# A four-layer gated stack: split fp32r scores for the eight-headed layer, weights of two stages in the streamed buffer, and a new common order of steps

## What is computed

```python
x = x + tanh(g_xattn[0]) * L0_xattn(layernorm(x), ctx)    # 32 heads of 8, differential softmax
x = x + tanh(g_ffn[0])   * L0_ffn(layernorm(x))           # three cycles of a small coupling net
x = x + tanh(g_xattn[1]) * L1_xattn(ctx, layernorm(x), mask)
x = x + tanh(g_ffn[1])   * L1_ffn(layernorm(x))           # 2 shared and 8 routed experts
x = x + tanh(g_xattn[2]) * L2_xattn(layernorm(x), ctx, ctx)
x = x + tanh(g_ffn[2])   * L2_ffn(layernorm(x))           # attention, then 8 experts
x = x + tanh(g_xattn[3]) * L3_xattn(layernorm(x), ctx, ctx)
x = x + tanh(g_ffn[3])   * L3_ffn(layernorm(x))           # quantised weights
```

```python
sim = einsum('bhid,bhjd->bhij', q * scale, k) * scale
sim = where(full_mask, sim, max_neg); attn = softmax(sim); out = attn @ v; out = layernorm(out @ Wo)
```

## Time and profile before

| | us |
|---|---|
| median of 3 runs | 5636.66 (5631.06 to 5639.46) |
| the profiled execution's own time | 5660.27 |
| its span, first to last instruction | 5658.5 |
| PE busy | 4888.0 (86%) |
| DVE busy | 2758.3 (49%) |
| ACT busy | 1853.5 (33%) |
| mean granted TensorE clock | 0.921 of full |

### The profile page before, as it was taken

The page is one execution under the profiler, slowest core; times in us unless marked ns, Lnnn a source line. Parts: engine busy times, 40 slices in busy tenths (PEclk is TensorE's granted clock), DMA queues, the critical chain, the costliest instruction groups (busy, mean ns, idle before and its releaser), DMA issues.

```text
span 5658.5 us, 74258 instructions
## 1 busy us (share of the span) xinstructions
PE 4888.0 (86%) x29184; PEld 3477.8 (61%) x29184; DVE 2758.3 (49%) x7346; ACT 1853.5 (33%) x3068; POOL 95.5 (2%) x180
## 2 busy tenths in 40 slices
PE   2898878989799897998979988899888998889988
PEld 1556765567656685565855658556585565855657
DVE  3535455354553545436454454544545445454454
ACT  2422324233242333423233242332424324242242
POOL 0000000000000000000000000000000000000000
PEclk9898989999899898998989989799897998989989
DMA  6000210002000020000200002000020000200002
GB/s 273 1 1 22 88 50 1 1 22 112 26 1 1 22 112 26 1 9 21 105 26 1 15 23 97 26 1 14 31 90 26 1 22 23 90 26 1 22 23 94
DMA packets 47155, 218.95 MB, mean 39 GB/s; under 512 B 4544, under 2 KB 16832, under 8 KB 27072
## 3 DMA queue, kind: packets, MB, share of 16 engines
q1 hardware_dynamic: 46784, 213.90, 10.2%
HBM read 192.91 MB, written 20.97 MB: 38 GB/s over the span
## 4 chain that ended last, share of the span: by engine, by line
PE 70%; DVE 19%; ACT 5%; issue 3%; DMA 2%; SPq 0%; POOL 0%; DVEq 0%; ACTq 0%
PE w L418 16%; PE w L428 10%; DVE mx L1023 6%; PE o L559 6%; PE w L675 6%; PE w L517 5%; PE w L667 4%; PE w L408 4%; PE w L531 4%; PE o L552 4%; PE w L484 2%; ACT oth L786 2%; PE w L534 1%; PE w L571 1%; PE w L467 1%
## 5 line engine op out<-in xcount | busy, mean ns | idle before, releaser
L824 ACT ACTIVATE pt<-w 128x1024 f32<-128x1024 f32 x640 | 653.8, 1024 | 768.6 <-PE w L534 440.4
L1023 DVE TENSOR_REDUCE mx<-w 128x4 f32<-128x1024 f32 x512 | 593.7, 1218 | 171.9 <-PE w L467 155.1
L559 PE MATMUL o<-pt,va 128*32 128x256 f32 x4096 | 559.5, 410 | 18.7 <-ACT pt L824 18.7
L786 ACT ACTIVATE oth<-w,res 128x256 f32<-128x256 f32 x656 | 264.1, 475 | 731.0 <-PE w L667 599.8
L1259 DVE TENSOR_REDUCE mx<-w 128x2 f32<-128x1024 f32 x128 | 156.9, 1226 | 527.0 <-PE w L519 527.0
L418 PE MATMUL w<-xnT,res 128*128 128x256 f32 x1408 | 375.3, 418 | 33.8 <-ACT xnT L778 24.5
L667 PE MATMUL w<-qsp,ksp 128*128 128x256 f32 x2048 | 350.3, 289 | 0.0
L418 PEld LDWEIGHTS w<-xnT,res 128*128 128x128 f32 x1408 | 281.3, 208 | 98.8 <-issue 47.6
L559 PEld LDWEIGHTS o<-pt,va 128*32 128x32 f32 x4096 | 207.9, 114 | 194.1 <-issue 67.8
L467 PE MATMUL w<-ksp,qsp 32*128 32x256 f32 (+1 forms) x2048 | 260.9, 401 | 73.5 <-DVE mx L1023 41.5
L418 PE MATMUL w<-xnT,stream 128*128 128x256 f32 x1280 | 311.8, 391 | 0.0
(11 more groups left out here) (235 smaller groups left out, 7506.6 us busy)
## 6 DMA issues: line engine op xcount, KB each, us to landing
stream_lo<-split SPq DMA_DIRECT2D x64, 1024.0 KB, 4.8
ksp<-split SPq DMA_DIRECT2D x64, 1024.0 KB, 6.9
stream<-in_moe_dram SPq DMA_DIRECT2D x80, 384.0 KB, 3.6
va<-in_moe_dram SPq DMA_DIRECT2D x8, 1024.0 KB, 10.3
split<-ksp SPq DMA_DIRECT2D x8, 1024.0 KB, 5.6
split<-qsp SPq DMA_DIRECT2D x8, 1024.0 KB, 8.0
res<-in_resident_dram SPq DMA_DIRECT2D x1, 8157.5 KB, 22.1
cx<-in_ctx_dram SPq DMA_DIRECT2D x16, 256.0 KB, 3.6
```

What stands on the lines that cost most here:

```text
L559: mm = pe.matmul(o[g:g + 32, 0:T], by_heads(plan, s)[:, kt, plan.v_of(h), :], pt[:, n % EXPS, a * 512 + kt * T:a * 512 + (kt + 1) * T], st ...
L786: h = act.activation(dst[:, c, :], w[:, c * T:(c + 1) * T], func, bias=bias[:, c:c + 1], **more)
L824: act.activation(pt[:, n % EXPS, :], w[:, :], ACT.Exp, scale=scale).then_inc(S["s_P"], 1)
L1023: dve.tensor_reduce(mx[s][:, :, 2 * u:2 * u + 2].rearrange("p t a -> p a t"), w[:, :].rearrange("p (a t k) -> p a t k", a=2, t=TT), AX_X, ...
```

## The change: what it does

Three things at once.

**Scores of L1.** `q` and `k` are split into a high part (rounded to fp32r) and the rest. For each head, `k1` now holds 128 rows: 64 of high and 64 of low parts (for odd heads the other way round). `qsp` holds the high part of `q` twice, and the low part stands in `hl` (even heads) or `qodd` (odd heads) beside 64 rows of zeros. Two fp32r matmuls of 128 rows take the place of each fp32 matmul. The mask's row and the row of ones become 128-row tiles with zeros in the others (`first_row`, `maskb`). The copies out of PSUM work on 64 partitions at a time: ACT does four for `q` and two each for `kc` and `kl`; DVE then does two subtractions for each, and one memset for `q`. `max` waits for the DVE parts.

**Where weights lie.** `l1_wkv`, `l1_wq` and `l1_wo` (2 MB) leave `res` and are loaded into `stream` in every pass, behind `cx` and ahead of `x` in SP's queue. f1's first five experts go to `stream` when the L1 steps that read the place are done in both slots. `f3_w1` (1 MB) is loaded into `stream` when the last f2 experts are done in both slots, and `f3.h` waits for it.

**The order.** `l1.q` comes after `l1.kl` and `l1.vl`, and `ORDER` is another string. Waits for a reused bank or exponential buffer, so far by count, now name the step that read that buffer. ACT's part of `l3.k` now also waits for the same slot's last `f2.exp`, and PE's `l1.kl` for `l1.xT`.

The core of the diff:

```diff
-    "1016110156106000006006000005000600050550550005000500050500000550050550500500505050005000500555055055"
...
+    "1666166016015151000500000500005000000000000505005005005050500505050050500000500505005005505505500555"
+    "5005555055555550555555555050550205552050500550002205507500005500055505505050705555005505077005050005"
+    "0055050500555000055050000050055555050005555550550550555555550500050505080085055555550005555000555500"
+    "0500500585355503303000080500050550050005005050050055000505005505505505555005050055550005555555505000"
+    "0550505050505000000050500500500505050500555050005555055545055505555509050555505055055050500550505050"
+    "055005555055900005055450055500500050"
...
+        + steps_of(s, "f0.add", "l1.ln", "l1.xT", "l1.kl", "l1.vl", "l1.q") + scores(L1, s) + values(L1, s)
...
                     for tt in range(TT):
-                        pe.matmul(w[:, tt * 512:(tt + 1) * 512], qz[s][:, u, tt * P:(tt + 1) * P],
-                                  k1[s][:, u // 2, :], start=True, stop=False)
-                        mm = pe.matmul(w[:, tt * 512:tt * 512 + T], ones_row[:, 0:P], maskb[s][:, :], start=False, stop=True)
+                        for n, q in enumerate((qsp[s][:, u, :], q_low(s, u))):
+                            pe.matmul(w[:, tt * 512:(tt + 1) * 512], q[:, tt * P:(tt + 1) * P], k1[s][:, u, :],
+                                      start=(n == 0), stop=False)
+                        mm = pe.matmul(w[:, tt * 512:tt * 512 + T], first_row[:, 0:P], maskb[s][:, :], start=False, stop=True)
...
                     for kt in range(KT):
                         o = w[:, kt * T:(kt + 1) * T]
-                        pe.matmul(o, k1[s][:, u // 2, kt * P:(kt + 1) * P], qz[s][:, u, :], start=True, stop=False)
+                        for n, q in enumerate((qsp[s][:, u, :], q_low(s, u))):
+                            pe.matmul(o, k1[s][:, u, kt * P:(kt + 1) * P], q, start=(n == 0), stop=False)
                         if kt < TT:
-                            pe.matmul(o, maskb[s][:, kt * P:(kt + 1) * P], ones_row[:, :], start=False, stop=False)
+                            pe.matmul(o, maskb[s][:, kt * P:(kt + 1) * P], first_row[:, :], start=False, stop=False)
                         mm = pe.matmul(o, sel1[:, u, :], mT[s][:, :], start=False, stop=True)
...
                     elif step == "l1.q":
                         w = full(act, step, s)
-                        for half in range(2):
-                            h = act.activation(qz[s][:, half::2, :], chunks_of(w, 4), ACT.Copy, scale=W_["half"][:, half:half + 1])
-                        h.then_inc(S["s_qz"], 1)
+                        full(act, "l1.cT", s)
+                        for odd in range(2):
+                            for rows in range(2):
+                                h = act.activation(qsp[s][64 * rows:64 * rows + 64, odd::2, :],
+                                                   chunks_of(w, 4)[64 * odd:64 * odd + 64], ACT.Copy)
+                        h.then_inc(S["s_qhi"], 1)
                     elif step in ("l1.kc", "l1.kl"):
-                        evac(k1[s][:, :, o:o + T], chunks_of(full(act, step, s), 4), "s_k1")
+                        for odd in range(2):
+                            r = slice(64 * odd, 64 * odd + 64)
+                            h = act.activation(k1[s][r, odd::2, o:o + T], chunks_of(w, 4)[r], ACT.Copy)
+                        h.then_inc(S["s_k1hi"], 1)
...
+                    elif step == "l1.q":
+                        w = full(dve, step, s)[:, :].rearrange("p (c t) -> p c t", t=T)
+                        full(dve, "l1.vc", s)
+                        dve.memset(q_lows(s, 0)[64:128].bitcast(F32), 0.0)
+                        dve.wait_ge(*after("s_qhi", step, s))
+                        for odd in range(2):
+                            r = slice(64 * odd, 64 * odd + 64)
+                            h = dve.tensor_tensor(q_lows(s, odd)[r], w[r], qsp[s][r, odd::2, :].bitcast(F32), ALU.subtract)
+                        h.then_inc(S["s_qz"], 1)
+                    elif step in ("l1.kc", "l1.kl"):
...
+                        dve.wait_ge(*after("s_k1hi", step, s))
+                        for odd in range(2):
+                            r, other = slice(64 * odd, 64 * odd + 64), slice(64 - 64 * odd, 128 - 64 * odd)
+                            h = dve.tensor_tensor(k1[s][other, odd::2, o:o + T], w[r], k1[s][r, odd::2, o:o + T].bitcast(F32), ALU.subtract)
+                        h.then_inc(S["s_k1"], 1)
...
+                sp.dma_start(stream[:, :], resident_in[:, RESIDENT_COLS:RESIDENT_COLS + LATE_COLS]).then_inc(S["s_l1w"], 16)
                 sp.wait_ge(s_out, 16 * SLOTS)
...
+                sp.dma_start(stream[:, 0:2048], resident_in[:, RESIDENT_COLS + LATE_COLS:]).then_inc(S["s_f3w"], 16)
```

More of the change, by code:

```diff
@@ L55 @@
     ("l3_wq", 512), ("l3_wk", 512), ("l3_wv", 512), ("l3_bq", 2), ("l3_bk", 2), ("l3_bv", 256),
[1 row of a table removed]
[1 row of a table added]
 ]
+LATE = [("l1_wkv", 2048), ("l1_wq", 1024), ("l1_wo", 1024)]
+LAST = [("f3_w1", 2048)]
 RESIDENT_COLS = sum(n for _, n in RESIDENT)
+LATE_COLS = sum(n for _, n in LATE)
+RESIDENT = RESIDENT + LATE + LAST
 STAGE = [("sel8q", 256), ("sel8k", 256), ("sel16q", 256), ("sel16k", 256), ("sel1", 1024), ("f3_w2", 2048)]
@@ L238, in build @@
         at, W_ = 0, {}
-        for name, n in RESIDENT:
+        for name, n in RESIDENT[:-len(LATE + LAST)]:
             W_[name] = res[:, at:at + n]
@@ L262, in build @@
         stream_lo = over("stream_lo", [P, STREAM_COLS])
+        W_["f3_w1"] = stream[:, 0:2048]
+        late, at = {}, 0
+        for name, n in LATE:
+            W_[name] = stream[:, at:at + n]
+            late[name] = (at, at + n)
+            at += n
         pt = sb("pt", [P, EXPS, 1024])
@@ L276, in per_slot, with shared @@
             return [sb(f"{name}{s}", shape, dt) for s in range(SLOTS)]
-        def shared(name, shape, dt, name2, shape2):
+        def shared(name, shape, dt, name2, shape2, dt2=F32):
             first, second = [], []
@@ L501, in attention1 @@
                     o = 0 if what == "kc" else T
-                    if what == "kc":
-                        pe.wait_ge(*after("s_kvT", "l1.cT", s))
+                    pe.wait_ge(*after("s_kvT", "l1.cT" if what == "kc" else "l1.xT", s))
                     filled(by_features(take("l1." + what, s), mat("l1_wkv", FC), kvT[s][:, :, o:o + T], 0, 4))
@@ L542, in values_by_exps @@
                 if plan.item_starts(u) and i >= 2:
-                    pe.wait_ge(S["s_oT"], i - 1)
+                    last, ls, lu = ITEM_STEPS[i - 2]
+                    pe.wait_ge(*after("s_oT", last, ls, lu + PLANS[last[:2]].units_per_item - 1))
                 if u == 0:
@@ L925, in _ @@
                         o = 0 if what == "q" else 2
+                        if what == "k":
+                            full(act, "f2.exp", s, F2.units - 1)
                         biased(qz[s][:, o:o + 2, :], full(act, step, s), W_["l3_b" + what], FC).then_inc(S["s_qk3"], 1)
@@ L1172, in _ @@
             dve.memset(onesf[:, :], 1.0)
-            dve.memset(ones_row[:, :], 1.0)
+            dve.memset(first_row[:, :], 0.0)
+            for s in range(SLOTS):
+                dve.memset(maskb[s][:, :], 0.0)
+                dve.memset(qodd[s][:, :, :].bitcast(F32), 0.0)
             dve.memset(mp[:, :, :], 0.0)
@@ L1188, in _ @@
                 once(dve.tensor_reduce(nlam[:, j:j + 1], tmp[:, 8 * j:8 * j + 8], AX_X, ALU.add))
+            once(dve.memset(first_row[0:1, :], 1.0))
             once(dve.tensor_scalar(subw[:, :], W_["subln"], 1.0 - LAMBDA_INIT, None, ALU.mult))
@@ L1256, in _ @@
                         signal(normalise(qz[s], cx[s]), "s_xt", step, s)
+                    elif step == "l1.q":
[8 more added lines that the diff above has]
+                    elif step in ("l1.kc", "l1.kl"):
+                        o = 0 if what == "kc" else T
+                        w = full(dve, step, s)[:, :].rearrange("p (c t) -> p c t", t=T)
+                        dve.wait_ge(*after("s_k1hi", step, s))
[3 more added lines that the diff above has]
+                        h.then_inc(S["s_k1"], 1)
                     elif step == "l1.max":
@@ L1385, in _ @@
         def _(sp):
[L1386 removed]
+            sp.dma_start(res[:, :], resident_in[:, 0:RESIDENT_COLS]).then_inc(s_res, 16)
             sp.dma_start(stream[:, :], stage_in).then_inc(s_stage, 16)
@@ L1425, in _ @@
                         used("f1.down", e - RING1)
+                    else:
+                        for name, steps in (("l1_wkv", ("l1.kc", "l1.vc", "l1.kl", "l1.vl")), ("l1_wq", ("l1.q",)), ("l1_wo", ("l1.out",))):
+                            if n * MOE1_COLS < late[name][1] and (n + 1) * MOE1_COLS > late[name][0]:
+                                for step in steps:
+                                    used(step, 0)
```

(4 more changed lines are left out.)

40 lines of the change are left out of this document (24 added, 16 removed), and 4 rows, old and new, of tables (RESIDENT, SIGNALS).

## The result

The kernel after takes **6834.4 us** (median; 6826.1 to 6840.7), the kernel before 5638.1 (5631.1 to 5650.0): 1.212 times as long, interval 1.209 to 1.214, or 1196 us more. The forecast was 6225, within a range of 5760 to 6600. The direction is right; the rise that was forecast, 587 us, is half of the measured one, and the value lies outside the range.

The account below looks back on a forecast made before the run. PE's in-order queue and its holes were taken to bound the kernel. Holes of 115 us a pass less 40 of matmuls gave 75, 598 in eight, less 8.3 of set-up: 6225 us on the median's scale, range 5760 to 6600.

Parts of the forecast that it names:

- What bounds the kernel: Whole span: PE's in-order queue; a hole opens where a result's return time (need) exceeds the PE work between (cover).
- PE work removed: L1 scores: 1.36 us saved per `max` step and 1.14 per `exp` step, together 40 us a pass.
- Holes: PE waits the new order opens, stretch by stretch: sum 115 us a pass, with 4 taken off in the f1 experts.
- the credit for f1's clock: f1 experts: 4 us a pass taken off, as this stretch now loses that at the half clock.
- The coupling net: f0 and the start of L1 up to `l1.max@0`: 36 us a pass more holes, from bare chains and `q`'s split.
- L2 and f2's attention: 13 us a pass more holes: L2's start -4, `f2.xT@0` +4, `cTr@1` +6, `back`, `oT`, `out`, `qs` as neighbours +7.
- ACT and DVE work: Splits of `q` and `k`: copy 1.02 us, subtraction 1.22, 64 partitions as long as 128; `q` ready 6.7 us behind PE.
- rival 4: Slower clock in f0, L3 and f3: 60 us at half speed, half on the path, +30 a pass, 6465; 15%.
- Rivals 1 to 3: Other work refills holes, 5309, 5%; only neighbouring expert pairs lose, 5589, 7%; half the holes remain, 5768, 13%.
- Rival 5: L1 scores save nothing, fp32r at 512 columns being slow, and weight loads lie in the open: 6545; 3%.
- rival 6: L1 mask matmuls: one row as cheap as 128, so widening the mask saves nothing: 6327; 5%.

## Why the prediction was wrong

- **What bounds the kernel:** right. PE in its written order, with needs and covers. The chain of the kernel after has 26% DVE for 19%, and every new wait of over 4 us was named beforehand.
- **PE work removed, 40 us:** right where it can be read: 0.60 and 0.46 for the 0.592 and 0.476 taken, and 38 a pass between the two kernels with the new order.
- **Holes, 119 before the credit for f1's clock:** right, 128, and by stretch within 4 us for all but one. The coupling net was 4 too high. L2 and f2's attention, forecast 13, had 26.8: this is the one badly sized stretch, 110 us of the 609 missing (the others were 39 too high together). `f2.cTr`, named there, came out as forecast (+6.3 in both slots), and so did `f2.xT` (+4.6 for 4); the start of L2 and the small waits of `qs`, `shift`, `exp` and `oT`, forecast -4 and +7, came to 15.9, with 3.0 of `l2.q@0` that no line named.
- **ACT and DVE work:** right in price (below).
- **The clock: the step that failed.** The main sum took PE's matmuls at the full clock and only rival 4 charged for a slower one, at 30 us a pass and with a chance of 15%. It cost 57.7 a pass, 462 in eight. The rival looked for the low clock in f0, L3 and f3; those stretches lost 15.3 and 7.5, 23 for its 30. What it missed are the others: the f2 experts (14.6, with PE busy for 79%), L2 and f2's attention (10.6) and L1 (8.6). It also let only half of the loss stand on the path, while the sum above needs all of it. And the f1 stretch was even credited with 4 us for a lower loss than today; it lost 2.0 more. With 57.7 in the place of 0, the forecast is 6225 + 462 + 32 for that credit, 6719; with 8 x 9 more holes it is 6790. Of the last 44, some 32 come from the scale: the forecast took the profiled execution to lie 23.6 above the median, and that of the kernel after lies 8.3 below it.
- **The rivals.** Rivals 1 to 3 (covers don't matter, only expert pairs lose, half the holes) are refuted by the sum of holes, and the first two by the order alone costing 1270 as well. Rival 5 is refuted by the 38 us of PE work saved, rival 4 was the right mechanism at half its size. On rival 6, the mask, the run with the full mask took 117 us off. The Trainium skill, "TensorE: Matmul & The Clock Gate", section "Why this matters for your kernels", has a single matmul with few rows take the time of one with 128. By that rule this run should have changed nothing; here the measurement decides against it.
- **Right in the sum, wrong in the account:** the new scores were to bring 320 less in any order. In the old order they bring 168 at best, and nothing as they stand. The holes came out near the forecast although it charged the needs of `q` (6.7) and the queues behind the splits of `kc` and `kl` to the new order: with the old scores in the new order these holes are missing (0.5, 0 and 0 us for 5.0, 3.6 and 3.8), so they come with the scores. That both parts stand in one kernel hid this; it was luck. The queue of `x` behind 2048 KB was charged to the pass start (+2.5), but the old scores with all weights resident have the same holes there (17.4 for 17.6), so in this order the load opened none.
- **Small slips:** 45 of holes less today's 10.4 is 35, not 36; a `k`'s need is 2 x 1.02 + 2 x 1.22 = 4.5, not 4.7; the memset, taken at 0.2, takes 0.91, beside ACT's copies; and no row gives f0's 47 busy us of 92 (the window of the coupling net has 105.8 of 155.9). None of these moves the result by more than 8 us.

## What to carry to other kernels

An order that opens holes on TensorE is paid twice: by the holes, and by the matmuls around them at half the clock. So price a hole with the granted clock of a stretch that already has such holes, not with its length alone. Where a wait can't be covered with work, idle matmuls in it may be worth their place (479, 122 and 115 us here in three kernels). And before a step is moved to serve as cover, see what it covers now.

## What the runs showed of the hardware

The copies and subtractions of 64 partitions, groups by shape in the kernel after (busy us, mean ns of one, idle before):

```profile
L926 ACT ACTIVATE qsp<-w 64x1024 fp32r<-64x1024 f32 x64 | 65.2, 1019 | 60.7 <-PE w L443 60.1
L1315 DVE TENSOR_TENSOR k<-w,k 64x1024 fp32r<-64x1024 f32 x64 | 78.2, 1222 | 353.3 <-ACT k L934 352.9
```

They take as long as those of 128 partitions (1025 and 1221 ns). Splitting the rows between two instructions doubled the time here, and most of `q`'s need of 6.7 us is made of that.

- A one-row bf16 matmul lengthened its group by 0.21 us (behind 256 columns) to 0.30 us (behind 512) more than one with 128 rows did.
- The granted clock fell to 0.87 in a stretch where PE was busy for 79% and no hole was longer than 3.8 us, and was 1.00 there once the holes held idle matmuls.
- At the lower of the two clock levels fp32r matmuls are slower as well. The first `l1.max` after its 5 us hole in the kernel after:

```profile
3693.82 0.77 PE L543 MATMUL w<-k,qsp 128*128 128x512 f32 x1 [5.01 <-issue]
3694.39 0.63 PE L543 MATMUL w<-k,hl 128*128 128x512 f32 x1
3694.82 0.44 PE L545 MATMUL w<-maskb,first_row 128*128 128x256 bf16 x1
```

The granted clock is 0.50 in this stretch. The second fp32r matmul takes 3694.82 - 3694.39 = 0.43, against 0.24 at the full clock.
